# Expert phase of an attention and mixture-of-experts kernel: rows transposed in two halves of TensorE's array, second-layer products of a pair in one PSUM bank

## Chip, cores and metric

The kernel runs on one core of a Trainium2 chip. The metric is the device time of one execution in microseconds; the median of three runs is given.

## What is computed

For 32 sequences of 256 rows of 256 numbers the reference computes a cross-attention layer with a residual, and then a layer of experts with a residual. Only the second bears on this change:

```python
x = x + attention(layernorm(x), ctx)          # 16 heads of 64, causal and masked
xn = layernorm(x)                             # 8192 rows of 256
e = argmax(xn @ router_w.T + router_b)        # one of 32 experts for each row
h = relu(xn @ w1[e] + b1[e])                  # 256 -> 64
x = x + relu(h @ w2[e] + b2[e])               # 64 -> 256
```

## The kernel before

The program has two blocks. The first one does the attention, sequence by sequence, and routes: every row is written, by an indirect DMA, to a place in a list in main memory, so that each tile of 128 rows of the list belongs to one expert. It takes the first 1480 us or so. The second block is the expert phase, the only part that the diff touches.

The expert phase works on 48 pairs of tiles (256 rows a pair). `U = 8` sets of buffers are used in turn, and the set number is `u`; `u % 2` chooses between two PSUM buffers of each kind. Pairs 0 to 7 and the last 8 are written out, the 32 between them are a hardware loop of 4 rounds (`pairs_of`). Each engine has its own stream, tied to the others by semaphores:

- SyncE loads a pair's rows (`XS`) from the list once the pair that used the buffers 8 pairs before has its result.
- VectorE normalises them (`norm_pair`, line 1128, result `XH`), copies one of the two first-layer weights (line 1143), and makes the result `Y` (`add_pair`, line 1138): the second-layer product out of PSUM, clamped at 0, plus the residual.
- TensorE transposes `XH` (`turn`, line 1227), multiplies with the first layer (`hid`, line 1238) and with the second (`y_of`, line 1248). Its order is `turn` of pair u+2, `hid` of pair u+1, `y_of` of pair u. In `turn` a pair has four transposes of 128x128, two for each tile.
- ScalarE copies the transposed rows out of PSUM (`xht`, line 1185, result `XHT`), applies bias and clamp to the hidden layer (`hidden`, line 1192, result `HT`) and copies the other first-layer weight (line 1180).
- GpSimd scatters the rows of `Y` to their places in the output, two indirect DMAs a pair (line 1094).

The expert number of a tile is only known at run time. `expert` (line 1079) loads it from `tile_row` in SBUF into a register of the engine; the profile shows that as TENSOR_LOAD, among the instructions of the engine's queue (PEldq is TensorE's). `y_of` does it twice a pair.

`wait_apart` (line 25) waits for a semaphore and, if the awaited value is in a register, adds 1 to a semaphore `passed` that nobody reads. PSUM has 8 banks of 128 x 512 numbers: `psS` and `psT` have two banks each, `psO`, `psW` and the two of `psR` one each. Before the change the transposes go to `psO` and `psW` by turns, the second-layer products to `psS` and `psT`, one tile to each bank.

Of the kernel before, what the change touches and what calls it, by code (L numbers as in the profile page):

```python
# [6 lines left out]
ACT = mybir.ActivationFunctionType  # L7
# [9 lines left out]
P = 128  # L17
# [12 lines left out]
def attention_moe(nc, x, ctx, mask, Wq, Wk, Wv, Wo, bo, router_w, router_b, w1, b1, w2, b2, out):  # L30
# [20 lines left out]
    with ExitStack() as es:  # L51
# [1018 lines left out]
        s_y = sem("y_ready")  # L1070
        s_done = [sem(f"tile_out{u}") for u in range(U)]

        psXT = [psO, psW]
        psH = psR
        psY = [psS, psT]
        out_rows = out.rearrange("b n d -> (b n) d")

        def expert(eng, j, t):
# [5 lines left out]
        with nc.Block() as block2:  # L1084
# [33 lines left out]
            @block2.vector  # L1118
            def _(dve):
                dve.wait_ge(s_te_pe, 1)  # L1120
                nc.vector.tensor_copy(own_row[:], psR[1][0:1, 0:P]).then_inc(s_or, 1)
                dve.wait_ge(s_or, 1)
                nc.vector.tensor_scalar(tile_row[:], own_row[:], E - 1, None, ALU.bitwise_and).then_inc(s_row, 1)

                def norm_pair(i, u):
                    dve.wait_ge(s_in[u], 16 * i + 16)
                    for t in range(2):
                        last = nc.vector.tensor_scalar(XH[u][:, t, :], XS[u][:, t, 0:D], XS[u][:, t, D:D + 1],  # L1128
                                                       XS[u][:, t, D + 1:D + 2], ALU.subtract, ALU.mult)
                    last.then_inc(s_xh, 1)  # L1130

                def add_pair(i, u, free):

                    if free:
                        wait_apart(dve, s_passed, s_done[u], 32 * i)
                    nc.vector.tensor_copy(tok[u][:], XS[u][:, :, D + 2])
                    dve.wait_ge(s_y_pe, U * i + u + 1)
                    nc.vector.scalar_tensor_tensor(out=Y[u][:], in0=psY[u % 2][:, :, 0:D], scalar=0.0,  # L1138
                                                   in1=XS[u][:, :, 0:D], op0=ALU.max, op1=ALU.add).then_inc(s_y, 1)

                def w1_copy(i, u):
                    e = expert(dve, U * i + u, 1)
                    nc.vector.tensor_copy(W1[u][:, 1, :], W1R[:, bass.ds(e, 1), :].rearrange("p a c -> p (a c)")
                                          ).then_inc(s_w1[1], 1)

                AHEAD = 3
                for u in range(U):
                    last = nc.vector.memset(HT[u][HID:HID + 1, :, :], 1.0)  # L1148
                last.then_inc(s_ht1, 1)
                dve.wait_ge(s_row, 1)  # L1150
                dve.wait_ge(s_w1r, 16)
                for u in range(AHEAD):
                    norm_pair(0, u)
                    w1_copy(0, u)

                def pairs_of(i, free, more):
                    for u in range(U):
                        if u + AHEAD < U:
                            norm_pair(i, u + AHEAD)
                            w1_copy(i, u + AHEAD)  # L1160
                        elif more:
                            norm_pair(i + 1, u + AHEAD - U)
                            w1_copy(i + 1, u + AHEAD - U)
                        add_pair(i, u, free)

                pairs_of(0, False, True)
                with dve.Fori(1, NP // U - 1) as i:
                    pairs_of(i, True, True)
                pairs_of(NP // U - 1, True, False)

            @block2.scalar
            def _(act):
                act.wait_ge(s_row, 1)
                act.wait_ge(s_b1r, 1)

                act.wait_ge(s_w1r, 16)

                def w1_copy(i, u):
                    e = expert(act, U * i + u, 0)
                    nc.scalar.activation(W1[u][:, 0, :], W1R[:, bass.ds(e, 1), :].rearrange("p a c -> p (a c)"), ACT.Copy  # L1180
                                         ).then_inc(s_w1[0], 1)

                def xht(i, u):
                    act.wait_ge(s_xh_pe, U * i + u + 1)
                    nc.scalar.activation(XHT[u][:].rearrange("p t c q -> p (t c q)"), psXT[u % 2][:, 0:2 * KD * P], ACT.Copy  # L1185
                                         ).then_inc(s_xht, 1)

                def hidden(i, u):
                    e = [expert(act, U * i + u, t) for t in range(2)]
                    act.wait_ge(s_h_pe, U * i + u + 1)  # L1190
                    for t in range(2):
                        last = nc.scalar.activation(HT[u][0:HID, t, :], psH[u % 2][half(t), 0:P], ACT.Relu,  # L1192
                                                    bias=B1T[half(t), bass.ds(e[t], 1)])
                    last.then_inc(s_h, 1)

                for u in range(2):
                    w1_copy(0, u)
                    xht(0, u)

                def pairs_of(i, more):  # L1200
                    for u in range(U):
                        hidden(i, u)
                        for f in (w1_copy, xht):
                            if u + 2 < U:
                                f(i, u + 2)
                            elif more:
                                f(i + 1, u + 2 - U)

                with act.Fori(0, NP // U - 1) as i:
                    pairs_of(i, True)  # L1210
                pairs_of(NP // U - 1, False)

            @block2.tensor
            def _(pe):
# [2 lines left out]
                pe.wait_ge(s_row, 1)  # L1217

                def turn(i, u, free=True):
                    pe.wait_ge(s_xh, U * i + u + 1)  # L1220
                    if free:
                        pe.wait_ge(s_xht, U * i + u - 1)
                    for t in range(2):
                        xh = XH[u][:, t, :].rearrange("p (d c) -> p c d", c=KD)
                        for c in range(KD):
                            o = (t * KD + c) * P
                            last = nc.tensor.transpose(psXT[u % 2][:, o:o + P], xh[:, c, :], ident[:])  # L1227
                    last.then_inc(s_xh_pe, 1)

                def hid(i, u, free=True):  # L1230
# [11 lines left out]
                def y_of(i, u, free=True):  # L1242
                    e = [expert(pe, U * i + u, t) for t in range(2)]
                    if free:
                        pe.wait_ge(s_y, U * i + u - 1)
                    pe.wait_ge(s_h, U * i + u + 1)
                    for t in range(2):
                        last = nc.tensor.matmul(psY[u % 2][:, t, 0:D], HT[u][:, t, :],  # L1248
                                                W2R[0:HID + 1, bass.ds(e[t], 1), :].rearrange("p a d -> p (a d)"),
                                                start=True, stop=True)  # L1250
                    last.then_inc(s_y_pe, 1)
# [48 lines left out]
```

## Time and profile before

| what | before |
|---|---|
| median of 3 runs (lowest to highest) | 1627.81 us (1627.48 to 1628.41) |
| the profiled execution | 1630.46 us |
| its span, first to last instruction | 1628.7 us |
| TensorE busy over the span | 1546.2 us (95%) |
| VectorE, ScalarE, GpSimd busy over the span | 75%, 61%, 20% |
| mean granted clock of TensorE | 0.982 |

Times within the profile are counted from the start of the span. The span is 1.8 us shorter than the time of the same execution. Busy shares are averages over both blocks; the attention block sets most of them. GpSimd's 20% is 10% in the attention slices and 70% or more in the last ones.

### The profile page before, as it was taken

The numbers are of one execution on the slowest core, as the hardware profiler recorded it, in microseconds if no ns is written. First come the engines' busy times: TensorE is split into PE (matmuls) and PEld (weight loads), VectorE is DVE, ScalarE is ACT, GpSimd is POOL, SyncE is SP. The second block draws the span as 40 slices with busy tenths as digits, with TensorE's granted clock in tenths as the row PEclk, the third lists the DMA queues.
The fourth block names the chain that finished last, engine by engine and source line by source line (L and its number), as shares of the span: only waits on it lengthen the run. The fifth ranks groups of instructions, "written<-read, shape, count | busy, mean of one in ns | idle before, by whom it ended". The sixth has DMA issues, their size and how long they took to land. (4 is left out here: it accounts for less than half of the span.)

```text
span 1628.7 us, 42357 instructions
## 1 busy us (share of the span) xinstructions
PE 1546.2 (95%) x12452; PEld 1266.9 (78%) x12453; DVE 1213.6 (75%) x5249; ACT 995.3 (61%) x3110; POOL 333.1 (20%) x505
## 2 busy tenths in 40 slices
PE   4989999999999999999999999999999999984885
PEld 4878888888888888888888888888888888873664
DVE  5668777777777787777787777787777778774663
ACT  4656666666666666656666666666666666652663
POOL 1111111111111111111111111111111111112776
PEclk9999999999999999999999999999999999996997
DMA  7750000000000000000000000000000000003761
GB/s 220 200 176 27 27 20 27 27 20 27 20 27 20 27 26 27 22 25 27 20 26 26 21 21 26 27 26 27 20 27 27 20 27 14 13 21 105 208 181 36
DMA packets 69294, 77.67 MB, mean 48 GB/s; under 512 B 10983, under 2 KB 63373, under 8 KB 69265
## 3 DMA queue, kind: packets, MB, share of 16 engines
q1 hardware_dynamic: 61010, 60.17, 13.2%
q0 software_dynamic: 7680, 16.93, 3.0%
q8 instruction: 13, 0.21, 0.1%
q10 hardware_dynamic: 576, 0.23, 0.0%
q14 instruction: 15, 0.12, 0.0%
HBM read 47.61 MB, written 33.88 MB: 50 GB/s over the span
## 5 line engine op out<-in xcount | busy, mean ns | idle before, releaser
L692 ACT ACTIVATE Sm<-Sm,mneg 128x128 f32<-128x128 f32 (+1 forms) x1024 | 456.0, 449 | 369.3 <-DVE mneg L937 368.8
L937 DVE CUSTOM_DVE_ANT_0 Sm<-psS,MK 128x128 f32<-128x128 f32 (+1 forms) x1024 | 304.4, 353 | 136.1 <-PE psS L544 127.1
L544 PE MATMUL psS<-KT,QT 64*128 64x128 f32 (+1 forms) x2048 | 238.5, 351 | 4.1 <-DVE mneg L937 2.6
L569 PE MATMUL psO<-PT,V 128*64 128x256 f32 (+1 forms) x2048 | 223.6, 339 | 2.4 <-ACT PT L685 2.0
L555 PE MATMUL psT<-ident,Sm 128*128 128x128 f32 x1536 | 225.3, 283 | 0.0
L569 PEld LDWEIGHTS psO<-PT,V 128*64 128x64 f32 x2048 | 124.6, 136 | 124.4 <-issue 84.9
L685 ACT ACTIVATE PT<-psT 128x768 f32<-128x768 f32 x256 | 204.5, 799 | 1.1 <-PE psT L555 0.8
L555 PEld LDWEIGHTS psT<-ident,Sm 128*128 128x128 f32 x1536 | 164.1, 141 | 44.5 <-issue 43.9
L692 ACT ACTIVATION_READ_ACCUMULATOR Sm<-Sm,mneg 128x1 f32 x1024 | 196.4, 192 | 0.0
L954 DVE SCALAR_TENSOR_TENSOR Sm<-Sm,halve,rinv 128x512 f32<-128x512 f32 x256 | 193.0, 754 | 0.0
L419 POOL DMA_INDIRECT lists<-stg,lrow x64 | 67.9, 1061 | 588.9 <-DVE lrow L894 579.2
L544 PEld LDWEIGHTS psS<-KT,QT 64*128 64x128 f32 x2048 | 134.9, 187 | 59.2 <-issue 43.9
L654 ACT ACTIVATE QT<-psR 128x512 f32<-128x512 f32 x128 | 76.0, 593 | 119.0 <-PE psR L474 116.6
L668 DVE COPY V<-psR 128x512 f32<-128x512 f32 x128 | 88.2, 689 | 69.1 <-PE psR L474 69.1
L951 DVE SCALAR_TENSOR_TENSOR Sm<-Sm,halve,rinv 128x256 f32<-128x256 f32 x256 | 124.5, 486 | 5.8
L474 PE MATMUL psR<-CT_hi,Wk_hi 128*128 128x256 f32 x512 | 114.6, 306 | 0.0
L474 PE MATMUL psR<-XT_hi,Wq_hi 128*128 128x256 f32 x512 | 106.8, 291 | 7.9 <-DVE Wq_lo L1018 7.9
L959 DVE TENSOR_TENSOR OT_lo<-psO,OT_hi 128x256 fp32r<-128x256 f32 x256 | 106.4, 416 | 1.0 <-ACT OT_hi L700 1.0
L474 PE MATMUL psR<-XT_lo,Wq_hi 128*128 128x256 f32 x512 | 103.9, 285 | 0.0
L474 PE MATMUL psR<-CT_lo,Wk_hi 128*128 128x256 f32 x512 | 103.8, 284 | 0.0
L474 PE MATMUL psR<-CT_hi,Wk_lo 128*128 128x256 f32 x512 | 103.7, 285 | 0.0
L1094 POOL DMA_INDIRECT out<-Y,tok x96 | 94.1, 980 | 46.2 <-issue 27.4
(156 smaller groups left out, 2938.6 us busy)
## 6 DMA issues: line engine op xcount, KB each, us to landing
lists<-pad SPq DMA_DIRECT2D x8, 1560.0 KB, 16.2
XS<-lists SPq DMA_DIRECT2D x48, 260.0 KB, 3.0
x_in<-in_x SPq DMA_DIRECT2D x32, 256.0 KB, 2.7
ctx_in<-in_ctx SPq DMA_DIRECT2D x32, 256.0 KB, 2.7
xr<-in_x SPq DMA_DIRECT2D x32, 256.0 KB, 2.6
W2R<-in_L_ffn_weights SPq DMA_DIRECT2D x1, 2048.0 KB
out<-Y,tok POOLq DMA_INDIRECT x96, 3.0
W2R<-in_L_xattn_Wq SPq DMA_DIRECT2D x1, 1024.0 KB, 9.3
```

What stands on the lines that cost most here:

```text
L474: last = nc.tensor.matmul(dst, a(k), z(k), start=(n == 0), stop=(n == 3 * len(ks) - 1))
L544: last = nc.tensor.matmul(psS[:, side, o:o + (it + 1) * P], QT[rows, p, it * P:(it + 1) * P], KT[rows, p, 0:(it + 1) * P], start=True, sto ...
L555: last = nc.tensor.transpose(psT[:, side, i * P:(i + 1) * P], Sm[:, p % 4, side, src:src + P], ident[:])
L569: last = nc.tensor.matmul(psO[DH * side:DH * side + DH, t * P:N], V[:, t, DH * h:DH * h + DH], PT[:, side, cols], start=(t == 0), stop=(t ...
L668: nc.vector.tensor_copy(V[:, i % 2, 512 * (i // 2):512 * (i // 2) + 512], src[:, :]).then_inc(s_v, 1)
L685: nc.scalar.activation(PT[:], psT[:, :, 0:384], ACT.Copy).then_inc(s_pt, 1)
L692: nc.scalar.activation(v, v, ACT.Exp, bias=mneg[:, p % 2, k:k + 1], scale=-1.0, accum_out=rsum[:, p % 2, k:k + 1]).then_inc(s_exp, 1)
L937: nc.vector.tensor_tensor_reduce(out=Sm[:, p % 4, side, cols], in0=psS[:, side, cols], in1=MK[:, cols], scale=-SCALE, scalar=3e38, op0=ALU ...
L951: nc.vector.scalar_tensor_tensor(out=v, in0=v, scalar=halve[:, 0:1], in1=of[:, :, 0:1].broadcast_to([P, 2, P]), op0=ALU.mult, op1=ALU.mult ...
L954: nc.vector.scalar_tensor_tensor(out=v, in0=v, scalar=halve[:, 1:2], in1=of[:, :, 1:2].broadcast_to([P, 2, N]), op0=ALU.mult, op1=ALU.mult ...
L959: nc.vector.tensor_tensor(OTl[:, p, :], psO[:, 0:N], OTh[:, p, :], ALU.subtract).then_inc(s_o, 1)
L1094: nc.gpsimd.indirect_dma_start(out_rows, bass.IndirectOffsetOnAxis(ap=tok[u][:, t:t + 1], axis=0), Y[u][:, t, :], None, bounds_check=last_ ...
```

## The change

The two kinds of PSUM buffers change places: the transposes now go to `psS` and `psT` with two banks each, the second-layer products to `psO` and `psW` with one bank each, where the two tiles of a pair lie side by side. Each transpose of 128 rows is split in two: rows 0 to 63 in the upper half of TensorE's array into the first bank, rows 64 to 127 in the lower half into the second bank. A pair has eight transposes with 64 rows loaded and 64 columns of the identity moved. ScalarE reads both banks in one instruction and puts the halves together. The two waits at the head of `turn` are made with `wait_apart`.

```diff
-        psXT = [psO, psW]
+        psXT = [psS, psT]
         psH = psR
-        psY = [psS, psT]
+        psY = [psO, psW]
...
-                    nc.vector.scalar_tensor_tensor(out=Y[u][:], in0=psY[u % 2][:, :, 0:D], scalar=0.0,
+                    nc.vector.scalar_tensor_tensor(out=Y[u][:], in0=psY[u % 2][:].rearrange("p (t d) -> p t d", t=2), scalar=0.0,
                                                    in1=XS[u][:, :, 0:D], op0=ALU.max, op1=ALU.add).then_inc(s_y, 1)
...
-                    nc.scalar.activation(XHT[u][:].rearrange("p t c q -> p (t c q)"), psXT[u % 2][:, 0:2 * KD * P], ACT.Copy
+                    nc.scalar.activation(XHT[u][:].rearrange("p t c (h q) -> p h (t c) q", h=2),
+                                         psXT[u % 2][:, :, 0:2 * KD * HID].rearrange("p h (b q) -> p h b q", q=HID), ACT.Copy
                                          ).then_inc(s_xht, 1)
...
                 def turn(i, u, free=True):
-                    pe.wait_ge(s_xh, U * i + u + 1)
+                    wait_apart(pe, s_passed, s_xh, U * i + u + 1)
                     if free:
-                        pe.wait_ge(s_xht, U * i + u - 1)
+                        wait_apart(pe, s_passed, s_xht, U * i + u - 1)
                     for t in range(2):
                         xh = XH[u][:, t, :].rearrange("p (d c) -> p c d", c=KD)
                         for c in range(KD):
-                            o = (t * KD + c) * P
-                            last = nc.tensor.transpose(psXT[u % 2][:, o:o + P], xh[:, c, :], ident[:])
+                            o = (t * KD + c) * HID
+                            for h in range(2):
+                                last = nc.tensor.transpose(psXT[u % 2][:, h, o:o + HID], xh[half(h), c, :],
+                                                           ident[half(h), half(h)])
                     last.then_inc(s_xh_pe, 1)
...
-                        last = nc.tensor.matmul(psY[u % 2][:, t, 0:D], HT[u][:, t, :],
+                        last = nc.tensor.matmul(psY[u % 2][:, t * D:(t + 1) * D], HT[u][:, t, :],
```

## Rows read from the trace of the kernel before

**Rows 1.** Instruction groups; after the bar: busy us, mean ns, idle before and releasers.

```profile
L1094 POOL DMA_INDIRECT out<-Y,tok x96 | 94.1, 980 | 46.2 <-issue 27.4 <-DVE Y L1138 18.8
```

**Rows 2.** Timeline of GpSimd (POOL), expert phase: start us, us, what, idle before.

```profile
1497.47 0.97 POOL L1094 DMA_INDIRECT out<-Y,tok  x1 [17.26 <-DVE Y L1138]
...
1538.74 0.97 POOL L1094 DMA_INDIRECT out<-Y,tok  x1 [0.30 <-issue]
...
1545.13 0.97 POOL L1094 DMA_INDIRECT out<-Y,tok  x1 [0.30 <-issue]
...
1597.83 0.98 POOL L1094 DMA_INDIRECT out<-Y,tok  x1 [0.30 <-issue]
...
1618.27 0.97 POOL L1094 DMA_INDIRECT out<-Y,tok  x1 [0.30 <-issue]
```

**Rows 3.** Timeline of VectorE (DVE): results Y of pairs 0, 16, 39, 47.

```profile
1495.95 0.69 DVE L1138 SCALAR_TENSOR_TENSOR Y<-psS,XS 128x512 f32<-128x512 f32 x1 [2.61 <-PE psS L1248]
...
1536.16 0.69 DVE L1138 SCALAR_TENSOR_TENSOR Y<-psS,XS 128x512 f32<-128x512 f32 x1 [1.04 <-PE psS L1248]
...
1594.27 0.69 DVE L1138 SCALAR_TENSOR_TENSOR Y<-psT,XS 128x512 f32<-128x512 f32 x1 [0.89 <-PE psT L1248]
...
1612.01 0.69 DVE L1138 SCALAR_TENSOR_TENSOR Y<-psT,XS 128x512 f32<-128x512 f32 x1 [1.62 <-PE psT L1248]
```

**Rows 4.** Timeline of TensorE in the loop: matmuls (PE), weight loads (PEld), merged.

```profile
1539.70 1.13 PE L1248 MATMUL psS<-W2R,HT 65*128 x4 [0.17 <-issue]
...
1542.04 1.13 PE L1248 MATMUL psT<-W2R,HT 65*128 x4 [0.16 <-issue]
...
1542.79 0.65 PEld L1227 LDWEIGHTS psO<-ident,XH 128*128 128x128 f32 x4
1543.00 0.63 PE L1227 MATMUL psO<-ident,XH 128*128 128x128 f32 x4
...
1543.56 0.66 PE L1238 MATMUL psR<-XHT,W 128*64 128x128 f32 x8
...
1544.59 1.13 PE L1248 MATMUL psS<-W2R,HT 65*128 x4 [0.37 <-issue]
```

**Rows 5.** Line 1079, pairs from 1542.04 and 1544.59: ns min/median/max, first and last start.

```profile
L1079 PEldq TENSOR_LOAD <-tile_row x2: 300/402/505, 1542.8 to 1543.7; - x2
...
L1079 PEldq TENSOR_LOAD <-tile_row x2: 301/482/663, 1545.3 to 1546.4; - x2
```

**Rows 6.** Event instructions by line: TensorE's from 1542.04, VectorE's from 1512 to 1594.

```profile
L1222 PEldq EVENT_SEMAPHORE  x1: 51/51/51, 1542.3 to 1542.3; - x1
...
L1235 PEldq EVENT_SEMAPHORE  x1: 51/51/51, 1542.6 to 1542.6; - x1
...
L27 DVEq EVENT_SEMAPHORE  x32: 21/21/21, 1514.0 to 1592.7; - x32
```

**Rows 7.** Attention: timeline of TensorE, then the page's group of the same loads.

```profile
1303.21 0.61 PE L474 MATMUL psR<-Wv_hi,CT_lo 128*128 128x512 f32 x2
1303.76 0.52 PEld L544 LDWEIGHTS psS<-KT,QT 64*128 64x128 f32 x8 [0.35 <-issue]
1303.76 0.93 PE L544 MATMUL psS<-KT,QT 64*128 64x128 f32 x8
...
L544 PEld LDWEIGHTS psS<-KT,QT 64*128 64x128 f32 x2048 | 134.9, 187 | 59.2 <-issue 43.9
```

**Rows 8.** Timeline at the start of the expert phase.

```profile
1489.95 1.10 PE L1227 MATMUL psO<-ident,XH 128*128 128x128 f32 x4 [3.77 <-DVE XH L1128]
...
1491.09 0.60 ACT L1185 ACTIVATE XHT<-psO 128x512 f32<-128x512 f32 x1 [3.13 <-PE psO L1227]
...
1494.78 1.13 PE L1248 MATMUL psS<-W2R,HT 65*128 x4
```

**Rows 9.** Busy time by stretch: length, engines' busy us (instructions), granted clock, DMA share, GB/s.

```profile
1490.00:1494.00 4.00, 4.00 (x22) 3.01 (x22) 2.59 (x10) 1.92 (x5) 0.00 (x0) 0.50 0.95 317
1494.00:1495.00 1.00, 1.00 (x10) 0.83 (x10) 0.00 (x0) 0.85 (x3) 0.00 (x0) 0.76 0.05 17
```

## The prediction, made before the changed kernel ran

> **What bounds the kernel now.** I began with the page's costliest groups and asked which of them lie in the expert phase, because the diff touches nothing else. The phase fills the last 140 of 1628.7 us. Its costliest group is not on TensorE: it is the indirect DMA of line 1094, 96 issues on GpSimd of 0.98 us each [rows 1]. Of the 46.2 us that GpSimd sat idle ahead of them, 27.4 are its own issue time, and 18.8 are a wait for a result Y, nearly all of it the wait for the first.
>
> Next I read GpSimd's timeline. The first issue starts at 1497.47, and the first issue of the last pair, number 94 after it, at 1618.27 [rows 2]. That is 120.80 us / 94 = 1.285 us an issue, 0.97 of it busy and 0.30 the gap behind it, or 2.57 us a pair. The same spacing holds at every row of that view. So from its first issue to its last GpSimd never stands: the phase ends when GpSimd has worked off 96 issues, and the span ends some 9 us after the last of them starts.
>
> Is GpSimd late because results are late? The timeline of VectorE gives the ends of Y (start plus 0.69) [rows 3]. I number the pairs 0 to 47. Pair 0 is ready at 1496.64 and issued at 1497.47, so 0.83 us is what the hand-over costs when GpSimd is waiting. Pair 16 is ready at 1536.85 and issued at 1538.74: 1.89 us, 1.06 more than needed. Pair 39 has 1597.83 - 1594.96 - 0.83 = 2.04 us to spare, and pair 47 has 1618.27 - 1612.70 - 0.83 = 4.74. This spare time is the cover behind which everything that I cost at nothing is hidden.
>
> What sets TensorE's own pace? Between its second-layer products (line 1248) lie 2.34, then 2.55 us [rows 4]. In the array the products take 0.96 (1542.04 to 1543.00), the transposes 0.56 (to 1543.56), the hidden layer 0.66 at most, together 2.18. The rest is its queue of instructions. The view by source line shows two loads of the tile's expert number in each pair. In the 2.55 us pair they took 300 and 505 ns; in the next pair, which is 2.70 us long, 301 and 663 ns [rows 5]. Take both to 300 and either pair is 2.34 us: 2.55 - 0.205, 2.70 - 0.36. So TensorE is held by its queue at 2.34 us, and stalled loads add the remainder. The 663 ns one begins at 1545.3 and ends at about 1546.0, inside the GpSimd issue that runs from 1545.13 to 1546.10 [rows 2]. From pair 16 to pair 39 TensorE needs (1594.27 - 1536.16) / 23 = 2.53 us a pair, close to GpSimd's 2.57, although its free pace is faster. My reading is that a TensorE that gets ahead runs into stalls that GpSimd's issues cause, and so is held near their pace.
>
> **The change, part by part.**
>
> *Half-height transposes.* Each of four transposes of 128x128 becomes two, with 64 rows loaded and 64 columns moved. I price them by the scores of attention (line 544), which have this shape: eight loads of 64x128, alternating between the halves of the array, took 0.52 us together, though one takes 187 ns, which makes 1.50 for eight in a row [rows 7]. The two halves therefore load side by side, and eight half-height loads cost as four steps. Now four steps take 0.56. The loads set the step, so halving the moved columns saves at most half of the last one, some 0.05 us.
>
> *One more change of tile shape.* Now the products and the transposes both use the full height, and the first transpose's load starts 0.21 us ahead of its matmul, under the last product (1542.79 against 1543.00) [rows 4]. In attention, where full height is followed by half height, the loads start only when the matmuls before have all but ended: 1303.76 against a modelled end of 1303.21 + 0.61 = 1303.82 [rows 7]. Applied here, the loads start at 1542.04 + 1.13 - 0.06 = 1543.11, take 0.52, and the hidden layer follows about 0.1 later, at 1543.7 instead of 1543.56. That is +0.14 us a pair in the array: 2.18 becomes 2.32, still under the queue's pace. It costs nothing while the queue and GpSimd are slower; uncovered it would cost 48 x 0.14 = 6.7 us.
>
> The Trainium skill, "TensorE: Matmul & The Clock Gate", section "LDWEIGHTS (loading the stationary operand)", says that a load's time goes by its columns and not by its rows. By this rule alone eight loads of 128 columns would take 8 x 107 = 853 ns instead of 427, +0.43 us a pair. The rows of line 544 say that the halves overlap, and I follow them; the rule left alone is the second rival.
>
> *The two waits of `turn` become waits with a count.* VectorE has this helper at line 27: one event instruction a pair, 32 of them in the loop, wait and count in one [rows 6]. Now `turn` shows one event (line 1222), its second wait riding on a load; afterwards it has two. Three of the queue's events (lines 1222, 1233, 1235) follow one another from 1542.3 to 1542.6, so they stand 0.1 to 0.2 us apart, though each takes 51 ns [rows 6]. I take 0.12 us for the one that is added; the bounds are 0.05 (its own length) and 0.24 (if two are added). Behind it wait the transposes, the hidden layer and the next loads. It touches only the 32 pairs of the loop, since a wait for a constant adds no count. The eight more loads and matmuls add nothing that I can bound from a row except by the same reasoning: line 544 issues eight with no visible queue time.
>
> So the queue's free pace goes from 2.34 to 2.46, still under 2.57. What is late next? If stalls give the 0.12 back, nothing. If they give none back, pair 39 is ready 32 x 0.12 = 3.8 us later, less the 2.04 to spare: +1.8 us at the end.
>
> *Banks.* ScalarE reads the same 512 elements from two banks, VectorE reads Y's 512 from one bank instead of two; I take both unchanged, 0 us, by element count. If either took 0.1 longer it would lie under the same cover. The buffers stay two deep.
>
> *The start.* Here TensorE is at half clock: 0.50 until 1494, rising within the next microsecond [rows 9]. The first four transposes took 1.10 us, XHT starts as they end (1491.09), and the products of pair 0 at 1494.78 [rows 8]. At half clock the moved columns set the step: (1.10 - 0.46) / 3 = 0.21. With half the columns it is about 0.11, so each set of four is some 0.3 to 0.4 shorter, less about 0.1 for a change of shape. The chain to the first Y holds two or three such sets, partly on ScalarE's queue. I take 0.4 earlier; bounds 0 and 0.8. This is the one gain that reaches the end, because GpSimd starts with the first Y and then never stands.
>
> **Sum.** Start -0.4, GpSimd's 96 issues 0, tail 0: -0.4 us. The profiled execution took 1630.46 us around a span of 1628.7, 0.16% above the median 1627.81; I apply the difference to the median: 1627.4. With the bounds of the start and of the added event (-0.8 and +1.8) the forecast's own range is 1627.0 to 1629.6. A measurement of this kernel can hardly tell 0.2%, or 3.3 us, from no change.
>
> **Rivals.**
>
> 1. *TensorE's queue becomes the bound (slower).* It decides once the loop's pace passes 2.57 us. Two events instead of one: 32 x 0.24 = 7.7, less 2.04 to spare and 0.4 at the start: +5.2, or 1633. If the counting event also waited until the products before it had started, it would be worse. For: TensorE's 2.53 is close. Against: part of 2.53 is stall, and VectorE's event takes 21 ns. Chance 0.08.
> 2. *The half-height loads run one after another (slower).* The source of XH is read with a step of two elements, that of line 544 is not. Eight steps of 0.14 instead of four: 2.32 + 0.56 = 2.88 us a pair. The last Y would end at 1495.95 + 47 x 2.88 + 0.69 = 1632.0, and its issue start 0.83 later, at 1632.8 instead of 1618.27: +14.5, or 1642. By the rule of loads alone, with 0.43 in place of 0.56, it would be 6 us less. Chance 0.04.
> 3. *The clock rises later (same or slower).* The transposes keep TensorE busy for less time, so the rise near 1494.5 could come one pair or so later; a pair at half clock costs up to 2 x 2.18 = 4.4 instead of 2.34, so about +1.5 in all: 1629.3. For: only 5 us of work precede the rise. Against: from 1495 on the array would still be busy most of each pair. The same page's section on transposes says that they don't count as activity for the clock; by that nothing changes here, and no row can show it. Chance 0.05.
> 4. *TensorE does bound the phase (faster).* Chains through the phase pass over TensorE. If the shorter moved columns saved 0.1 to 0.2 a pair, 48 pairs give up to 10 us: 1618. Against it stand 94 even intervals of GpSimd. Chance 0.03.
>
> **From these to the numbers.** My forecast holds 0.80. Within 0.2% lie the forecast and rival 3: 0.84 with a little taken off for their tails. Slower: rivals 1 and 2 and those tails, 0.13. Faster: rival 4, 0.03. The range must leave out no more than 2 in 10: 1626.6 (the start's full gain and some spread) to 1630.6 (no stall given back, or a late clock, with spread).
>
> **What would show it.** Right: 96 issues of line 1094 still 1.28 us apart, the first at about 1497.1; line 1227 as 384 matmuls with eight loads spanning 0.5 to 0.6 us; hidden layer 1.65 us after the products (now 1.52); one more event a pair on TensorE's queue at line 27; loads of the expert number stalled less in sum; spare time smaller than now at pair 39 but above 0. Wrong: gaps over 0.3 on GpSimd in the middle of the phase with Y as releaser (rival 1 or 2, told apart by the span of the eight loads), or half clock after 1495 (rival 3).

## The result and the profile after

| | before | after |
|---|---|---|
| median (lowest to highest) | 1628.07 us (1627.48 to 1628.41), 4 runs | 1681.98 us (1680.4 to 1684.06), 4 runs |
| the profiled execution, its span | 1630.46, 1628.7 | 1681.9, 1680.2 |
| mean granted clock of TensorE | 0.982 | 0.934 |

The changed kernel is slower by 3.3%: the ratio is 1.0327, 95% interval 1.0315 to 1.034. The forecast was 1627.4, its range 1626.6 to 1630.6. The prediction was wrong, and by more than any of its rivals. Two executions further down lost far more clock than the others of their kernel and stand in no ratio: one of the kernel before took 2177.43 us at a mean clock of 0.641 (third group, unexplained), and one of `e13` took 1691.45 us at 0.930.

The first thing to read in the page after is GpSimd's group, the answer to [rows 1], and the row of the granted clock in 40 slices (42 us each):

```profile
PEclk9999999999999999999999999999999999955555
...
L1094 POOL DMA_INDIRECT out<-Y,tok x96 | 93.4, 972 | 100.9 <-DVE Y L1138 86.0
```

GpSimd's own work is what it was (93.4 us for 94.1), but its idle time has grown from 46.2 to 100.9 us, and now VectorE's `Y` ends most of it. The last five slices, which are the expert phase, have half the clock. The windows say when. First the kernel after, then the kernel before (stretch, length, busy us of PE, PEld, DVE, ACT and POOL, granted clock, DMA share, GB/s):

```profile
1440.00:1460.00 20.00, 16.70 (x149) 13.02 (x149) 16.27 (x80) 12.00 (x38) 1.86 (x2) 1.00 0.03 8
...
1470.00:1480.00 10.00, 0.31 (x5) 0.21 (x5) 4.52 (x31) 0.00 (x0) 2.04 (x2) 0.50 0.08 27
...
1490.00:1495.00 5.00, 5.00 (x36) 3.61 (x36) 2.10 (x7) 3.19 (x8) 0.00 (x0) 0.50 0.22 77
1495.00:1500.00 5.00, 5.00 (x28) 3.31 (x25) 1.89 (x8) 2.17 (x7) 2.91 (x3) 0.50 0.41 118
1500.00:1520.00 20.00, 20.00 (x107) 12.88 (x107) 7.85 (x26) 8.74 (x22) 10.70 (x12) 0.50 0.49 151
...
1640.00:1675.00 35.00, 27.40 (x137) 17.93 (x136) 10.73 (x32) 10.22 (x25) 17.83 (x19) 0.50 0.05 10
```

```profile
1470.00:1480.00 10.00, 2.18 (x13) 1.94 (x13) 5.06 (x34) 0.00 (x0) 1.83 (x2) 0.50 0.04 14
...
1495.00:1500.00 5.00, 4.93 (x36) 4.01 (x36) 3.27 (x10) 3.54 (x9) 1.95 (x2) 1.00 0.29 79
1500.00:1520.00 20.00, 17.57 (x131) 13.90 (x130) 13.17 (x40) 13.08 (x32) 15.39 (x16) 1.00 0.75 213
```

In both kernels the clock falls to 0.50 (1.2 GHz) when attention ends and TensorE has little to do. Before, it is back at 1.00 (2.4 GHz) by 1495 [rows 9] and stays there while TensorE has work. After, it never comes back: 0.50 in every stretch to the end. Note the PE column: after, TensorE is "busy" for 20.00 of 20.00 us and the clock stays down; before, 17.57 of 20.00, and it stays up. The profile's busy time alone does not tell whether the clock will rise.

What a pair costs at that clock is read from the timeline of TensorE, the answer to [rows 4]:

```profile
1549.94 0.56 PEld L1229 LDWEIGHTS psS<-ident,XH 64*128 64x128 f32 x8 [0.65 <-issue]
...
1549.94 0.74 PE L1229 MATMUL psS<-ident,XH 64*128 64x64 f32 x8
1550.62 1.12 PE L1241 MATMUL psR<-XHT,W 128*64 128x128 f32 x8
1551.83 2.07 PE L1251 MATMUL psO<-W2R,HT 65*128 x4
1553.83 0.74 PE L1229 MATMUL psT<-ident,XH 64*128 64x64 f32 x8
1554.50 1.12 PE L1241 MATMUL psR<-XHT,W 128*64 128x128 f32 x8
1555.56 0.79 PE L1251 MATMUL psW<-W2R,HT 65*128 x1
```

From products to transposes 2.00 us, to the hidden layer 0.67, to the next products 1.06: 3.73 us a pair, with no gap. The array is the bound. GpSimd, which did not stand before [rows 2], now waits ahead of the first issue of every pair but the last:

```profile
1495.32 0.98 POOL L1094 DMA_INDIRECT out<-Y,tok  x1 [17.58 <-DVE Y L1138]
...
1566.63 0.97 POOL L1094 DMA_INDIRECT out<-Y,tok  x1 [1.48 <-DVE Y L1138]
1567.91 0.97 POOL L1094 DMA_INDIRECT out<-Y,tok  x1 [0.30 <-issue]
1570.42 0.97 POOL L1094 DMA_INDIRECT out<-Y,tok  x1 [1.53 <-DVE Y L1138]
...
1669.79 0.97 POOL L1094 DMA_INDIRECT out<-Y,tok  x1 [0.30 <-issue]
```

The results of the first and the last pair, beside [rows 3]:

```profile
1493.80 0.69 DVE L1138 SCALAR_TENSOR_TENSOR Y<-psO,XS 128x512 f32<-128x512 f32 x1 [2.90 <-PE psO L1251]
...
1667.44 0.69 DVE L1138 SCALAR_TENSOR_TENSOR Y<-psW,XS 128x512 f32<-128x512 f32 x1 [0.94 <-PE psW L1251]
```

That closes the sum. The last `Y` comes at 1667.44 instead of 1612.01, 55.4 us later. Before, GpSimd was 4.74 us behind it; now 1669.79 - 1668.13 - 0.83 = 0.83 us. 55.4 - 3.9 = 51.5 us, which is the difference of the spans (1680.2 - 1628.7) and that of GpSimd's first issue of the last pair (1669.79 - 1618.27).

### The profile page after: what moved, and what is told of

It is laid out like the page before. It is cut to its first block and busy times, and to the rows that moved or that the text cites. A ratio compares the mean times of both kernels' runs of the same rounds, so it can differ in the third digit from the quotient of the medians.

```text
span 1680.2 us, 42781 instructions
## 1 busy us (share of the span) xinstructions
PE 1615.6 (96%) x12644; PEld 1298.0 (77%) x12645; DVE 1210.2 (72%) x5249; ACT 995.2 (59%) x3110; POOL 332.2 (20%) x505
## 5 line engine op out<-in xcount | busy, mean ns | idle before, releaser
L1094 POOL DMA_INDIRECT out<-Y,tok x96 | 93.4, 972 | 100.9 <-DVE Y L1138 86.0
```

Source lines behind the costliest of these rows:

```text
L1094: nc.gpsimd.indirect_dma_start(out_rows, bass.IndirectOffsetOnAxis(ap=tok[u][:, t:t + 1], axis=0), Y[u][:, t, :], None, bounds_check=last_ ...
```

## The experiments

The questions were which part of the change takes the clock, and what is left of the difference when the clock is there. Each run is compared with runs of the kernel before on the same chip.

**First group.** On this chip the kernel before itself took 1686.3 us (1683.08 to 1689.51, 27 runs) at mean clocks of 0.933 to 0.937, so these four runs say what a kernel does that is at half clock for most of the phase.

`e1_counting_waits`, the kernel before with the new waits alone:

```diff
 def turn(i, u, free=True):
-    pe.wait_ge(s_xh, U * i + u + 1)
+    wait_apart(pe, s_passed, s_xh, U * i + u + 1)
     if free:
-        pe.wait_ge(s_xht, U * i + u - 1)
+        wait_apart(pe, s_passed, s_xht, U * i + u - 1)
```

> The kernel before with only the two waits of turn made counting waits (one more event instruction a pair on TensorE's queue). Theory A (the lighter half-height transposes keep the clock at 0.50; the waits are innocent): 1627 to 1630, clock 1.00 from 1495 on, 96 issues on GpSimd 1.28 us apart. Theory B (the waits or their gaps hold the clock down or make TensorE's queue the bound): over 1633, and if the clock stays at 0.50 over 1670.

Measured: 1688.16 us, ratio 1.001 (1.0001 to 1.002). Its windows show that the clock came and went:

```profile
1495.00:1500.00 5.00, 4.79 (x36) 3.84 (x35) 3.15 (x10) 3.39 (x9) 2.26 (x3) 1.00 0.39 85
...
1503.00:1505.00 2.00, 0.76 (x4) 0.73 (x4) 2.00 (x7) 1.28 (x3) 0.64 (x1) 0.80 0.03 8
1505.00:1510.00 5.00, 5.00 (x26) 3.50 (x24) 2.36 (x8) 1.94 (x5) 3.25 (x4) 0.50 0.74 207
```

TensorE stood for 1.24 of the 2 us in which the clock fell. The stall is 1.77 us long and ends at 1504.24, with a late `XH` as its releaser:

```profile
1504.24 1.13 PE L1227 MATMUL psO<-ident,XH 128*128 128x128 f32 x4 [1.77 <-DVE XH L1128]
```

After that its full-height pairs took 3.91 us each (products at 1541.54 and 1545.45) and the clock did not rise again. So a kernel with full-height transposes and products over 65 rows can stay at half clock too, once it has lost it. Neither theory can be read from a chip on which the kernel before is at half clock as well.

`e2_banks_only`, the kernel before with the two kinds of PSUM buffers exchanged, transposes still at full height into one bank:

```diff
-        psXT = [psO, psW]
+        psXT = [psS, psT]
-        psY = [psS, psT]
+        psY = [psO, psW]
...
-   last = nc.tensor.transpose(psXT[u % 2][:, o:o + P], xh[:, c, :], ident[:])
+   last = nc.tensor.transpose(psXT[u % 2][:, 0, o:o + P], xh[:, c, :], ident[:])
```

> The kernel before with only the PSUM banks exchanged: full-height transposes into the first bank of psS and psT, second-layer products of a pair in one bank. Theory A: 1627 to 1629, clock and issues as before. Theory B (two products in one bank, or reads of it, slow the pair and with it the clock): a longer time between products than 2.53 us in the loop and over 1633.

Measured: 1687.37 us, ratio 1.0007 (0.9997 to 1.0016), with the clock lost as in `e1`; TensorE stood for 1.46 us, until 1503.62, while it fell. On this chip neither run decides; `e13` below repeats the two together where the kernel before keeps its clock.

`e3_warm_start`, the changed kernel with ten more matmuls of 128 columns ahead of the first transposes:

```diff
 pe.wait_ge(s_row, 1)
+for _ in range(10):
+    nc.tensor.matmul(psH[0][:, 0:P], ident[:], ident[:], start=True, stop=True)
```

> The changed kernel with ten matmuls of 128x128 by 128 columns (identity by identity, result unused) put into the wait ahead of the first transposes, so that the clock rises before the first pair. Theory A1 (only the rise is missing, half-height pairs hold a clock that is up): clock 1.00 from about 1490 to the end, first Y 1 to 2 us earlier than before, 1626 to 1629. Theory A2 (half-height pairs do too little in the array even to hold it): the clock falls back to 0.50 within the phase, 1665 to 1682.

Measured: 1683.38 us, ratio 0.9976 (0.9965 to 0.9986). The clock does rise, ahead of 1491, and falls again near 1497.4, some 7 us later:

```profile
1492.00:1497.00 5.00, 4.20 (x44) 3.04 (x44) 2.20 (x8) 3.40 (x10) 0.00 (x0) 1.00 0.30 104
1497.00:1500.00 3.00, 2.83 (x17) 1.88 (x18) 1.23 (x5) 2.00 (x6) 1.95 (x2) 0.56 0.46 132
```

So a missed rise is not all of it: on this chip the changed pairs don't hold the clock either. Nor do full-height ones here (`e1`, `e2`), so whether the half-height pairs are to blame is left to `e12`.

`e4_first_pairs_full`, the changed kernel with full-height transposes for pairs 0 to 7 (`i` is 0, `split(i)` false) and halves from pair 8 on:

```diff
 for c in range(KD):
+    if not split(i):
+        o = (t * KD + c) * P
+        last = nc.tensor.transpose(psXT[u % 2][:, 0, o:o + P], xh[:, c, :], ident[:])
+        continue
     o = (t * KD + c) * HID
```

> The changed kernel with full-height transposes for pairs 0 to 7 (one bank) and half-height ones for pairs 8 to 47; ScalarE's first round of 8 pairs is written out. Theory A1: the clock rises near 1494.5 as before and stays, 1627 to 1630. Theory A2: it rises and falls again soon after 1513, where the half-height pairs begin; 1660 to 1675.

Measured: 1680.72 us, ratio 0.9964 (0.9947 to 0.9981). The clock fell before the first half-height pair, again at the end of a stall for a late `XH` (1.82 us, until 1503.23), so the run had to be made again elsewhere (`e12`). Beside the full-height pairs of `e1` at the same half clock, the half-height pair is the cheaper one: 3.73 us instead of 3.91.

**Second group**, on another chip; the kernel before took 1630.2 us (1628.17 to 1630.91, 7 runs).

`e5_after_again`: the changed kernel as it is.

> The changed kernel unaltered, next to the kernel before on the same chip, because the kernel before took 1628 on one chip and 1686 on another. Theory A (half-height transposes keep the clock from rising; whether a clock that has risen survives depends on the chip): clock 0.50 from 1467 on wherever it runs, 1680 to 1684; the ratio is 1.03 where the kernel before keeps its clock and about 0.997 where it loses it. Theory C (it was the chip that differed, not the kernel): ratio within 0.995 to 1.005 and the clock rises in both.

Measured: 1680.74 us, ratio 1.0313 (1.0291 to 1.0334), clock 0.50 in every window from 1470 to the end (mean clock of its four executions 0.931 to 0.941). The result comes again, beside the kernel before on the same chip.

`e6_before_full_rows` and `e7_after_full_rows`: `HT` gets 128 rows, of which the added ones hold zeros, and the second-layer products run over all 128 rows of the array instead of 65. They move the same columns in the same time. VectorE writes the zeros once, at the start of the block. The edit to the kernel before, and to the changed one:

```diff
-HT = [kept(f"HT{u}", [HID + 1, 2, P]) for u in range(U)]
+HT = [kept(f"HT{u}", [P, 2, P]) for u in range(U)]
...
+   last = nc.vector.memset(HT[u][HID:P, :, :], 0.0)
...
-   W2R[0:HID + 1, bass.ds(e[t], 1), :].rearrange("p a d -> p (a d)"),
+   W2R[:, bass.ds(e[t], 1), :].rearrange("p a d -> p (a d)"),
```

> The kernel before with the second-layer products made over 128 rows instead of 65 (rows 65 to 127 of HT are zero; same columns, same duration, same result). Theory A' (the clock goes by how many rows of the array work, not only by how long): the clock rises at the start and stays up or comes back, 1626 to 1630 on any chip. Theory D (rows don't count): as the kernel before on the same chip, 1628 or 1686.

> The changed kernel with second-layer products over 128 rows. Theory A': clock 1.00 for most of the phase, 1626 to 1632 on any chip; GpSimd's issues 1.28 us apart again. Theory D: as the changed kernel, 1680 to 1684.

Measured: `e6` 1632.61 us, ratio 1.0016 (1.0001 to 1.003); `e7` 1640.73 us, ratio 1.0067 (1.0052 to 1.0081). With nothing changed but the rows of the products and the clearing of the added ones, the half-height kernel has lost 40 us, and its clock is back. The clock is as theory A' has it; the time is 9 us over that theory's range. Windows and timeline of `e7`:

```profile
1495.00:1500.00 5.00, 4.49 (x40) 3.07 (x38) 3.10 (x10) 3.27 (x8) 1.95 (x2) 0.96 0.26 81
1500.00:1520.00 20.00, 17.13 (x144) 12.24 (x144) 11.59 (x37) 11.75 (x29) 14.58 (x15) 1.00 0.67 197
...
1560.00:1600.00 40.00, 31.66 (x278) 22.41 (x277) 22.36 (x70) 22.61 (x56) 26.42 (x28) 1.00 0.52 151
```

```profile
1550.59 1.12 PE L1256 MATMUL psO<-W2R,HT 128*128 x4 [0.51 <-issue]
1551.65 0.69 PE L1234 MATMUL psT<-ident,XH 64*128 64x64 f32 x8
1552.27 0.66 PE L1246 MATMUL psR<-XHT,W 128*64 128x128 f32 x8
1553.40 1.13 PE L1256 MATMUL psW<-W2R,HT 128*128 x4 [0.47 <-issue]
```

This run is also the first look at the changed pair at full clock. Its 2.81 us are over GpSimd's 2.57, and TensorE stands 0.47 us ahead of the products with "issue" as the reason: its queue is late. `e6` took 2.4 us more than the kernel before. In its profile TensorE sits idle for 6.08 us ahead of the first transposes, 3.77 in [rows 8], because VectorE clears 64 rows first (`e7` has the same 6.08 us); `e14` below moves that work away:

```profile
1489.92 1.10 PE L1232 MATMUL psO<-ident,XH 128*128 128x128 f32 x4 [6.08 <-DVE XH L1129]
```

`e8_half_twice`, the changed kernel with every half-height transpose made twice, products over 65 rows:

```diff
-    for h in range(2):
+    for h in (0, 1, 0, 1):
```

> The changed kernel with every half-height transpose made twice, so that a pair moves as many columns through each half as before the change. Theory A: the clock rises at the start of the phase, near 1495, as in the kernel before; then it lives or dies as that kernel's does on this chip (1628 to 1632, or 1684 to 1692). Theory E (the change of tile shape and its empty time before the transposes prevents the rise): no rise at all, 1686 or more, since the array has more to do.

Measured: 1685.01 us median of four that don't agree: 1654.74, 1683.54, 1686.47, 1687.09. The profiled execution is the 1654.74 one:

```profile
1490.00:1495.00 5.00, 5.00 (x65) 4.18 (x63) 2.55 (x10) 2.90 (x7) 0.00 (x0) 0.59 0.68 233
...
1600.00:1640.00 40.00, 36.53 (x352) 27.16 (x352) 20.19 (x62) 20.36 (x50) 25.88 (x28) 1.00 0.24 63
```

In that execution twice the transposes brought the clock up and kept it up for 140 us. The other three have a mean clock of 0.946 to 0.950, more than the 0.931 to 0.941 of `e5` on the same chip; they have no profile, so where in the phase the clock was up is not known. The 1654.74 us lie in neither theory's range. The Trainium skill ("TensorE: Matmul & The Clock Gate", Part 4: PE-mode transpose) says that transposes don't count as TensorE being busy for the clock in the same way as matmuls. By that, neither doubling them nor halving their columns should matter to the clock; here the one gave it back in one execution, the other lost it (`e12` and `e13` below), and the measurement decides.

**Third group**, another chip; the kernel before took 1629.48 us (median of 20 runs). The question was the queue: is it late in `e7` because eight transposes take longer to issue than four, or because of the added change of tile shape?

`e9_full_rows_full_twice` has eight transposes a pair as well, but all at full height (`e6` with each transpose made twice).

```diff
-    last = nc.tensor.transpose(psXT[u % 2][:, o:o + P], xh[:, c, :], ident[:])
+    for _ in range(2):
+        last = nc.tensor.transpose(psXT[u % 2][:, o:o + P], xh[:, c, :], ident[:])
```

> The kernel before with second-layer products over 128 rows and every full-height transpose made twice: as many instructions in turn as after the change (8 loads, 8 matmuls), but no change of tile shape between products and transposes. At full clock the changed kernel's second load of expert numbers starts 1.19 us after the products (before: 0.71 to 0.75) and its pair takes 2.8 us. Theory Q (TensorE's queue holds a limited number of waiting instructions, and the doubled transposes fill it): the first load of a pair starts 0.9 to 1.2 us after the products, pair 2.65 to 2.85, 1632 to 1642. Theory M (the added change of tile shape holds the queue back): it starts at 0.7 to 0.8, pair 2.57, 1630 to 1634.

Measured: 1632.1 us, ratio 1.0024 (1.0014 to 1.0035). First the timeline of TensorE in `e9`, then the first load of the expert number behind the transposes in `e9` and in `e7` (ns min/median/max, first and last start):

```profile
1552.09 1.13 PE L1254 MATMUL psS<-W2R,HT 128*128 x4
1553.06 1.11 PE L1233 MATMUL psW<-ident,XH 128*128 128x128 f32 x8
1554.10 0.66 PE L1244 MATMUL psR<-XHT,W 128*64 128x128 f32 x8
...
L1080 PEldq TENSOR_LOAD <-tile_row x1: 301/301/301, 1552.8 to 1552.8; - x1
```

```profile
L1080 PEldq TENSOR_LOAD <-tile_row x1: 299/299/299, 1551.8 to 1551.8; - x1
```

In `e9` the load starts 0.7 us after the products (1552.8 against 1552.09), ahead of the transposes' matmuls, though eight transposes stand in front of it in the queue. In `e7` it starts 1.2 us after them (1551.8 against 1550.59), when the first transpose has begun. So the number of transposes alone does not delay it; that is theory M's time for the load. But `e7` has two things that `e9` lacks, the change to halves and the two counting waits. `e13` below, with the waits and banks and full-height transposes, has the load 1.0 us after its products:

```profile
1547.16 1.13 PE L1248 MATMUL psW<-W2R,HT 65*128 x4 [0.52 <-issue]
...
L1079 PEldq TENSOR_LOAD <-tile_row x2: 298/303/308, 1548.2 to 1549.0; - x2
```

Its neighbours have 0.9. So about half of the delay (from 0.7 to 0.9 or 1.0 us) comes with the waits and banks, and the rest (to 1.2) with the change of height. The Trainium skill ("TensorEngine Tiling (Array Packing)", Key Properties) says that changing the tiling mode drains TensorE. The rows agree as far as they go: the half-height transposes start 1.06 us after the products in `e7` and the full-height ones 0.97 in `e9`, and the register load behind them is later still than in `e13`.

`e10_after_loads_early`: `e7` with both loads moved ahead of `turn`.

```diff
-    def y_of(i, u, free=True):
-        e = [expert(pe, U * i + u, t) for t in range(2)]
+    def y_of(i, u, e, free=True):
...
     for u in range(U):
+        e = [expert(pe, U * i + u, t) for t in range(2)]
```

> The changed kernel with products over 128 rows (as in the run that brought the clock back) and with a pair's two expert numbers loaded ahead of turn instead of behind hid. If the 10 us that are left are the loads that start late behind a full queue, as either theory Q or M has it: pair 2.57 again, GpSimd's issues 1.28 us apart, 1628 to 1633. If they are the array's own time or the counting waits: 1638 to 1642, unchanged.

Measured: 1636.1 us, ratio 1.0038 (1.0023 to 1.0053). That is 6.6 us over the kernel before on its chip, where `e7` was 10.5 us over: better, but not cured, and outside both theories' ranges. In the profiled execution the clock came only after 1500, and its loop pairs still took 2.5 to 3.1 us (products at 1539.89, 1542.98, 1545.54, 1548.05), with TensorE now standing ahead of the transposes (0.74 us before 1541.77, "issue"). But the clock, once up, stayed at 1.00 to the last products: these are half-height pairs with products over 128 rows, on the chip of `e12`.

`e11_before_rows_early_warm`: `e6` with the loads moved ahead and eight more matmuls at the start.

> The kernel before with products over 128 rows, expert numbers loaded ahead of turn, and eight 128x128 matmuls with an unused result in the wait ahead of the first transposes. Meant to beat both kernels: the clock is up at or before the first pair, the first Y comes 1 to 2 us earlier, GpSimd's 96 issues follow without a gap: 1626 to 1629 on a chip where the kernel before takes 1628 to 1630, and 1627 to 1632 where it takes 1686. If GpSimd's issues don't set the end at full clock, less than 1624.

Measured: 1631.81 us, ratio 1.0016 (1.0007 to 1.0026). No gain: GpSimd's issues bound it, and `XH` is late here too.

`e12_first_full_again`: the kernel of `e4`, where the kernel before keeps its clock.

> Full-height transposes for pairs 0 to 7, half-height for 8 to 47, products over 65 rows, as run on the first other chip; here the question is whether a chip on which the kernel before keeps its clock also keeps it with half-height pairs. Theory A1 (only the rise fails): clock 1.00 to the end, pair 2.8 us at full clock, 1636 to 1645. Theory A2 (half-height pairs can't hold it either): it falls after 1513, 1660 to 1680. On a chip where the kernel before takes 1686 it tells nothing new.

Measured: 1672.05 us, ratio 1.026 (1.0241 to 1.0279). The first half-height pair's transposes stand at 1505.63. Windows:

```profile
1510.00:1512.00 2.00, 1.98 (x18) 1.54 (x20) 0.94 (x4) 1.08 (x4) 1.65 (x2) 1.00 0.76 217
1512.00:1514.00 2.00, 1.26 (x11) 0.84 (x6) 1.09 (x4) 0.97 (x3) 1.39 (x3) 0.83 0.71 197
1514.00:1520.00 6.00, 6.00 (x37) 3.96 (x37) 2.98 (x8) 2.81 (x7) 3.81 (x4) 0.50 0.55 174
```

The clock had been at 1.00 for some 20 us and fell after three half-height pairs. From there most pairs took 3.73 us. TensorE had stood for 0.74 us just before; that stall alone doesn't explain the fall, since `e13` stood longer at about the same point of the phase and kept 1.00 (first `e12`, then `e13`):

```profile
1513.10 1.90 PE L1263 MATMUL psO<-W2R,HT 65*128 x4 [0.74 <-issue]
...
1511.45 0.91 PE L1248 MATMUL psO<-W2R,HT 65*128 x3 [0.83 <-ACT HT L1192]
```

**Fourth group**, a fourth chip; the kernel before took 1629.08 us (1626.22 to 1631.64, 27 runs).

`e13_waits_and_banks`: the kernel before with the edits of `e1` and `e2` together, which is the change without its half-height transposes.

> The kernel before with the change's counting waits and its exchange of banks, the transposes left at full height (one of 128 columns for each tile and 128-column block). Theory C (the loss is the clock, and the clock is lost by the half-height transposes): the granted clock rises near 1494 and holds through the expert phase as in the kernel before, and the time is within 3 us of it (1627 to 1632). Theory W (waits and banks together make the loss): the clock stays at 0.50 and the time is near 1680. Should this chip be one on which the kernel before loses its clock, the run tells nothing.

Measured: 1631.57 us, ratio 1.0013 (1.0003 to 1.0023), clock 1.00 in every window from 1495 to 1600. One of its ten executions took 1691.45 us at a mean clock of 0.930, so it lost the clock; the other nine lie within 1630.01 to 1633.39. So waits and banks together cost 0.5 to 3.7 us by the interval, and in nine of ten executions they leave the clock alone, where the changed kernel was without it in all eight of its own (mean clocks 0.931 to 0.941); the half-height transposes make that difference. Whether waits and banks make a loss likelier (one in ten, against none in 27 of the kernel before on this chip) these counts don't settle. In the profile GpSimd's first issue is at 1494.55 and that of the last pair at 1618.93:

```profile
1494.55 0.97 POOL L1094 DMA_INDIRECT out<-Y,tok  x1 [16.94 <-DVE Y L1138]
...
1618.93 0.97 POOL L1094 DMA_INDIRECT out<-Y,tok  x1 [0.30 <-issue]
```

That is 124.38 us for 47 pairs, 2.65 each instead of 2.57: GpSimd is no longer the bound all the way.

`e14_full_rows_gpsimd_clears`: `e6`, with GpSimd clearing the added rows and writing the row of ones; TensorE waits for them behind its first `hid`.

```diff
+   nc.gpsimd.memset(HT[u][HID:P, :, :], 0.0).then_inc(s_ht0, 1)
+   pool.wait_ge(s_ht0, U)
+   nc.gpsimd.memset(HT[u][HID:HID + 1, :, :], 1.0).then_inc(s_ht1, 1)
...
-   last = nc.vector.memset(HT[u][HID:HID + 1, :, :], 1.0)
```

> The kernel before with HT of 128 rows and products over all 128 rows, as in e6_before_full_rows, but GpSimd clears the added rows while VectorE does its work, so that the first XH is not late. Theory A (rows used in the products give the clock margin and cost no time of their own): the first XH comes about 2 us earlier than in e6_before_full_rows, the clock stays at 1.00 through the phase, and the time is 1626 to 1630, ratio 0.998 to 1.000. Theory Z (products over 128 rows cost time themselves): the ratio stays at 1.0016 or above, with the first issue of GpSimd no earlier.

Measured: 1628.35 us (1626.53 to 1630.39, 11 runs), ratio 0.9997 (0.9988 to 1.0006). Products over 128 rows cost no time of their own that these runs can tell. In the profiled execution the first transposes and the first issue come earlier than in `e6`:

```profile
1485.99 1.10 PE L1230 MATMUL psO<-ident,XH 128*128 128x128 f32 x4 [3.61 <-DVE XH L1134]
...
1493.43 0.98 POOL L1100 DMA_INDIRECT out<-Y,tok  x1 [6.61 <-DVE Y L1144]
```

`e15_same_with_six_more`: `e14` with six more matmuls at the start.

> e14_full_rows_gpsimd_clears with six more 128-column matmuls of ident on TensorE before the first transposes, so that the array is busy earlier. Theory A: the clock rises 2 to 5 us earlier than in e14_full_rows_gpsimd_clears and the first pair comes up to 1 us sooner, 1625 to 1629. Theory N (the start of the phase is set by the loads of the rows and not by the array): the same time as e14_full_rows_gpsimd_clears within 1 us, whatever the clock at the start.

Measured: 1628.62 us, ratio 0.9996 (0.9987 to 1.0006). Its clock was at 1.00 from 1490, and it gained nothing, as theory N has it. No version tried beats the kernel before by what can be measured.

## Why the prediction was wrong

**The step that failed** is the clock. "The start" took it for granted that the clock rises near 1494.5 as before, and rival 3, the only place where that was doubted, put its price at one more pair at half clock (+1.5 us), because "from 1495 on the array would still be busy most of each pair". It was busy all of each pair, and the clock never rose. From the first `Y` to the last the 47 intervals took 3.69 us on average (1493.80 to 1667.44) instead of 2.47 (1495.95 to 1612.01), 57.6 us more. Rival 3 doubted the right thing, the rise of the clock, but had it late by one pair and not lost for the phase; its sign, half clock after 1495, is what the windows show. I had priced each edit against the array's time and never against the clock that this time is counted in.

What the runs show in its place: with half-height transposes and products over 65 rows the clock neither rises (the changed kernel in its first runs and in `e5`) nor holds once up (`e12`; `e3` too, though on its chip nothing with products over 65 rows did). With the same transposes and products over 128 rows it does both (`e7`, `e10`). With full-height transposes, the new waits and the new banks it does both in nine executions of ten (`e13`). With more half-height transposes it does in one of four (`e8`). So in these runs the clock went with the height of the transposes and the rows of the products, and not with the time that TensorE is shown as busy. That the rows matter rests on two pairs of runs, `e5` and `e7` on one chip, `e12` and `e10` on another (these two differ also in the first eight pairs and in where the numbers are loaded); how the chip weighs them was not measured. Full-height transposes alone are no guarantee: on the first group's chip the clock was lost with them too.

**Half-height loads** run side by side: right. Eight take 0.56 us at half clock ([rows 7] had 0.52 at full clock), so rival 2 falls.

**One more change of tile shape**: the array's term was right, the queue's was not. I gave it +0.14 us in the array (2.32 a pair) and nothing in the queue (2.46 with the added event). At full clock, in `e7`, products to hidden layer is 1.68 us where I had 1.65, and the array needs 1.06 + 0.62 + 0.66 = 2.34. But the register loads behind the transposes start 1.2 us after the products instead of 0.7, and the pair is 2.81 us. That is rival 1, the queue as the bound, by the change of height as well as by the waits that it names. 47 x (2.81 - 2.57) = 11.3 us, and `e7` is 10.5 us slower than the kernel before. Some 2.4 us of that may be the clearing (`e6`). So had the clock held, the change would still have been slower; I estimate 1636 to 1641 from these differences, outside my range.

**Waits and banks**: priced at nothing behind cover, with +1.8 as the bound if no stall is given back. `e13` measures 1.0013, +2.1 us (0.5 to 3.7) for both together: near that bound, and the cover was not enough, since GpSimd's pairs became 2.65 us. Which of the two it is stays open. My reading that GpSimd's issues cause the long loads is not shown: in the kernel before, the loads at 1549.0 and 1551.7 also begin inside an issue (1548.97 to 1550.07, 1551.65 to 1552.68) and took 304 and 299 ns.

**The start**: the first transposes began 2.5 us earlier than before, which is not the change's doing: TensorE stood for the same 3.77 us ahead of them, and the matmul before that had ended 2.5 us earlier. From the first transposes to the first products, 4.83 us became 4.20 (1487.48 to 1491.68), 0.63 less where I took 0.4 with bounds 0 and 0.8; a set of four took 0.74 us instead of 1.10, as priced. It was lost at once, since those products ran at half clock (2.08 us for 1.13), and `Y` of pair 0 came 6.32 us after the first transposes instead of 6.00:

```profile
1487.48 0.74 PE L1229 MATMUL psS<-ident,XH 64*128 64x64 f32 x8 [3.77 <-DVE XH L1128]
...
1491.68 2.08 PE L1251 MATMUL psO<-W2R,HT 65*128 x4
```

**The bound**: GpSimd's issues do bound the kernel before, and `e14` and `e15` fit that from the other side: an earlier clock gives nothing. What I missed is how little lies between that bound and another state of the same kernel.

**Open.** Why the kernel before loses its clock on one chip, by the mean clock of all 27 runs, and keeps it on the others. The profiles give a hint: in `e1`, `e2` and `e4`, on that chip, TensorE stood for 1.77, 1.46 and 1.82 us some 10 us after the rise, and the clock fell during the stall or at its end; no profile of full-height pairs from another chip has a stall over 0.83 us between 1494 and 1512. What held the engines there, and whether it took the clock, was not tested. Whether the 128-row products of `e14` would hold it there was not tried; no later group ran on that chip.

## What to carry to other kernels

A change that makes TensorE's work smaller can cost its clock: ask of each phase at what granted clock it runs, when the clock rose, and whether the change makes the array's work lighter; price the whole phase at half clock as one rival, not one pair. If the clock is lost with TensorE shown as busy, look for matmuls that use part of the rows, pad them with zeros where that costs no time, and measure; here it worked on the two chips where it was tried with half-height transposes. And count a change of tile shape between matmuls, and an added wait, in the queue as well as in the array: the register loads behind them came later here.

## What was not expected of the hardware

- TensorE at half clock can be shown busy for 20.00 of 20.00 us and stay there for 180 us; the same loop with products over 128 rows instead of 65 is at 1.00 from 1496 on (1680.74 against 1640.73 us, same chip).
- The same kernel takes 1629 or 1686 us on different chips, at 0.981 to 0.986 and 0.933 to 0.937 as the mean clock over the span.
- Once fallen in the phase, the clock did not come back (`e1` to `e4`, `e12`): full-height pairs take 3.91 us, half-height ones 3.73.
- Eight full-height transposes instead of four, at full clock, make a pair 2.60 us (1552.09 to 1554.68), practically GpSimd's pace.
